# Block maxima of the weight quantiser by five halvings, exponents one chunk sooner, the step partly on ScalarE

## The reference, cut to what matters

```python
def _quant_elem(x, mbits):
    e = floor(log2(max(abs(x), 2**-30)));  e = max(e, 0)
    step = exp2(e - mbits)
    q = round(x / step) * step
    return clip(q, -max_norm, max_norm)

def _mx_quant(x, mbits):                      # weights: mbits = 1, max_norm = 6
    amax = max(abs(block of 32))
    shared_exp = floor(log2(amax)) - 2
    return _quant_elem(x / 2**shared_exp, mbits) * 2**shared_exp
```

## Time and profile before

| | |
|---|---|
| median of 3 runs | 1184.11 us (1183.37 to 1185.51) |
| profiled execution | 1184.98 us |
| its span | 1183.2 us |
| TensorE matmul busy | 1107.2 us (94%) |
| VectorE busy | 868.7 us (73%) |
| ScalarE busy | 606.5 us (51%) |
| GpSimd busy | 490.8 us (41%) |
| mean granted TensorE clock | 0.975 |

### The profile page before, as it was taken

The page is one execution under the profiler, slowest core; times in us unless marked ns, Lnnn a source line. Parts: engine busy times, 40 slices in busy tenths (PEclk is TensorE's granted clock), DMA queues, the critical chain, the costliest instruction groups (busy, mean ns, idle before and its releaser), DMA issues.

```text
span 1183.2 us, 17698 instructions
## 1 busy us (share of the span) xinstructions
PE 1107.2 (94%) x5878; PEld 885.2 (75%) x5878; DVE 868.7 (73%) x1471; ACT 606.5 (51%) x1236; POOL 490.8 (41%) x360
## 2 busy tenths in 40 slices
PE   3976868999999999999999999999899999999998
PEld 2433333477888888888888888887888989897887
DVE  6999989867867777786867777657666676765534
ACT  2523443545656556565656656553665565663110
POOL 1361000124555645564655645462656555550000
PEclk9797998999999999999999999999999999999999
DMA  9364135220010011101010010141103020111221
GB/s 324 129 199 166 45 126 194 89 85 18 19 56 29 23 53 31 53 18 58 18 58 27 22 35 14 63 123 54 55 19 83 28 55 35 48 36 72 71 106 71
DMA packets 41812, 83.10 MB, mean 70 GB/s; under 512 B 10211, under 2 KB 18916, under 8 KB 38564
## 3 DMA queue, kind: packets, MB, share of 16 engines
q1 hardware_dynamic: 40164, 77.24, 19.9%
q0 software_dynamic: 1600, 5.24, 1.4%
HBM read 71.59 MB, written 10.22 MB: 69 GB/s over the span
## 4 chain that ended last, share of the span: by engine, by line
PE 77%; DVE 11%; ACT 4%; issue 4%; DMA 2%; POOL 2%; SPq 1%; ACTq 0%; DVEq 0%; POOLq 0%
PE PS L1888 20%; PE PS L1890 20%; PE PS L1889 20%; PE PS L2037 10%; PE PS L1831 1%; PE PS L1674 1%; PE PS L1655 1%; ACT arena L970 1%; DVE blkamax L1177 1%; DMA arena<-in_ctx 1%; PE PS L1785 1%; PE PS L1725 1%; PE PS L1842 1%; DVE blkamax L1202 1%; DMA X<-in_x 1%
## 5 line engine op out<-in xcount | busy, mean ns | idle before, releaser
L674 POOL TENSOR_TENSOR arena<-arena,rsum 128x768 f32<-128x768 f32 x192 | 283.2, 1476 | 362.5 <-DVE rsum L1470 362.5
L985 ACT ACTIVATE PTH<-PS 128x384 fp32r<-128x384 f32 x384 | 167.7, 489 | 249.5 <-PE PS L2037 249.2
L1465 DVE TENSOR_REDUCE nmax<-PS 128x1 f32<-128x768 f32 x192 | 183.0, 954 | 116.2 <-PE PS L1890 115.0
L1515 DVE TENSOR_TENSOR PTL<-PS,PTH 128x384 fp32r<-128x384 f32 x384 | 194.5, 548 | 11.1 <-ACT PTH L985 10.4
L970 ACT ACTIVATE arena<-PS,nmax 128x768 f32<-128x768 f32 x192 | 174.2, 907 | 32.8 <-DVE nmax L1465 32.3
L2037 PE MATMUL PS<-identf,arena 128*128 128x128 f32 x1152 | 158.3, 273 | 5.8 <-POOL arena L674 3.6
L2037 PEld LDWEIGHTS PS<-identf,arena 128*128 128x128 f32 x1152 | 130.3, 140 | 9.3 <-POOL arena L674 4.4
L659 POOL TENSOR_TENSOR WQL<-arena,WQH 128x512 fp32r<-128x512 f32 x44 | 58.2, 1324 | 64.2 <-ACT WQH L744 64.2
L1888 PE MATMUL PS<-PTH,VSH 128*128 128x512 f32 (+1 forms) x198 | 81.1, 410 | 0.4 <-DVE X L1492 0.4
L1890 PE MATMUL PS<-PTH,VSL 128*128 128x512 f32 (+1 forms) x198 | 76.5, 386 | 0.0
L1888 PE MATMUL PS<-WOH,OTH 128*128 128x512 f32 (+1 forms) x180 | 74.7, 415 | 1.6 <-DVE OTL L1549 0.7
(11 more groups left out here) (289 smaller groups left out, 2540.9 us busy)
## 6 DMA issues: line engine op xcount, KB each, us to landing
arena<-in_wo SPq DMA_DIRECT2D x12, 1024.0 KB, 4.8
arena<-in_wq SPq DMA_DIRECT2D x44, 256.0 KB, 2.6
arena<-in_expert_w SPq DMA_DIRECT2D x8, 1024.0 KB, 4.8
arena<-in_wgu SPq DMA_DIRECT2D x11, 512.0 KB, 5.2
arena<-v_dram SPq DMA_DIRECT2D x8, 384.0 KB, 3.5
arena<-in_wd SPq DMA_DIRECT2D x4, 704.0 KB, 4.7
arena<-in_ctx SPq DMA_DIRECT2D x4, 512.0 KB, 4.0
arena<-in_ctx_t SPq DMA_DIRECT2D x2, 1024.0 KB, 10.6
```

The lines of the kernel that those rows point to most:

```text
L674: pool.tensor_tensor(PR[:, u % 4, :], PR[:, u % 4, :], rsum[:, u % 4:u % 4 + 1].broadcast_to([P, KEYS]), ALU.mult).then_inc(s["pn_ready"], 1)
L985: act.activation(fr(PTH[:, (u // 4) % 2, 3 * half:3 * half + 3, u % 4 * P:(u % 4 + 1) * P]), bank(B_PT[half])[:, 0:3 * P].rearrange("p (k ...
L1465: dve.tensor_reduce(nmax[:, slot:slot + 1], SC[pair][:, 0:KEYS], AX.X, ALU.max, negate=True)\
L1515: dve.tensor_tensor(fr(PTL[:, (u // 4) % 2, ks, cols]), bank(B_PT[half])[:, 0:3 * P].rearrange("p (k c) -> p k c", k=3), PTH[:, (u // 4) % ...
```

## The change

The reduce `weight_top` goes. `weight_halves` runs five times for a chunk (32 to 16, 8, 4, 2, 1); the fifth writes `block_top` and raises `amax_ready`. Halvings 0 to 4 of chunk c + 1 are laid around the shift, the rounding and the two caps of chunk c. The exponents of chunk c + 2 follow the fifth halving of chunk c + 1 and stand before its step and grid, so they are one chunk sooner than before. From chunk 5 on (`STEP_ON_ACT = 5`, the sixth chunk) ScalarE makes the step, ahead of the caps; for chunks 0 to 4 VectorE still does. In step 0, whose shift and rounding are done inside the layer norm, the exponents of chunk 1 still come first.

```diff
--- before.py
+++ after.py
@@ -328,6 +328,8 @@
 
         CONTEXT_LATE = ((10, 11, 12), (13, 14, 15))
 
+        STEP_ON_ACT = 5
+
         TAPS_AT = {9: 0, 10: 1, 11: 2, 12: 3}
 
         KPAIRS = KV1 // 2
@@ -346,8 +348,10 @@
         def tops(c):
 
             n, (t, _) = CHUNKS[c], chunk_blocks(c)
-            half, quarter = (top_scratch[int(c >= NCH)][:, a:b] for a, b in ((0, n // 2), (n // 2, 3 * n // 4)))
-            return [ap.rearrange("p (t e b) -> p t e b", t=t, e=MX >> i + 1) for i, ap in enumerate((half, quarter))]
+            scratch = top_scratch[int(c >= NCH)]
+            levels = [scratch[:, a:a + (n >> i + 1)] for i, a in enumerate((0, n // 2, 0, n // 2))]
+            return [ap.rearrange("p (t e b) -> p t e b", t=t, e=MX >> i + 1) for i, ap in enumerate(levels)]\
+                + [of_blocks(block_top[c % 2], c).unsqueeze(2)]
 
         def of_blocks(ap, c):
 
@@ -784,6 +788,9 @@
                 act.wait_ge(s["amax_ready"], c + 1)
                 if c >= 2:
                     act.wait_ge(s["wq8_ready"], c - 1)
+                if c >= STEP_ON_ACT:
+                    act.activation(of_blocks(block_step[c % 2], c), of_blocks(block_top[c % 2], c), ACT.Copy, scale=0.25)\
+                       .then_inc(s["step_ready"], 1)
                 for cap, sign in zip(block_caps[c % 2], (1.0, -1.0)):
                     act.activation(of_blocks(cap, c), of_blocks(block_top[c % 2], c), ACT.Copy, scale=1.5 * sign)\
                        .then_inc(s["caps_ready"], 1)
@@ -1194,24 +1201,18 @@
                 dve.scalar_tensor_tensor(w, weight_magic(c), ROUND / 2, w, ALU.mult, ALU.subtract)\
                    .then_inc(s["wx_shifted"], 1)
 
-            def weight_top(c):
-
-                if c >= 2:
-                    dve.wait_ge(s["caps_ready"], 2 * (c - 1))
-                dve.wait_ge(s["tops_ready"], 2 * c + 2)
-                dve.tensor_reduce(of_blocks(block_top[c % 2], c), tops(c)[1].rearrange("p t e b -> p t b e"),
-                                  AX.X, ALU.max).then_inc(s["amax_ready"], 1)
-
             def weight_halves(c, i):
 
-                src = tops(c)[0] if i else interleaved(weight_magic(c), c)
+                src = tops(c)[i - 1] if i else interleaved(weight_magic(c), c)
                 n = MX >> i + 1
                 if i:
-                    dve.wait_ge(s["tops_ready"], 2 * c + 1)
+                    dve.wait_ge(s["tops_ready"], 4 * c + i)
                 else:
                     dve.wait_ge(s["wexp_ready"], c + 1)
+                if i == 4 and c >= 2:
+                    dve.wait_ge(s["caps_ready"], 2 * (c - 1))
                 dve.tensor_tensor(tops(c)[i], src[:, :, 0:n, :], src[:, :, n:2 * n, :], ALU.max)\
-                   .then_inc(s["tops_ready"], 1)
+                   .then_inc(s["amax_ready" if i == 4 else "tops_ready"], 1)
 
             def weight_rounded(c):
 
@@ -1247,22 +1248,28 @@
             def weight_step(c, begun=False):
 
                 ahead = c + 1 < len(CHUNKS)
+                if begun:
+                    weight_exponents(c + 1)
                 if ahead:
-                    weight_exponents(c + 1)
+                    weight_halves(c + 1, 0)
                 if not begun:
                     weight_shifted(c)
                 if ahead:
-                    weight_halves(c + 1, 0)
+                    weight_halves(c + 1, 1)
                 if not begun:
                     weight_rounded(c)
                 if ahead:
-                    weight_halves(c + 1, 1)
+                    weight_halves(c + 1, 2)
                 weight_capped(c, 0)
                 if ahead:
-                    weight_top(c + 1)
+                    weight_halves(c + 1, 3)
                 weight_capped(c, 1)
                 if ahead:
-                    weight_least(c + 1)
+                    weight_halves(c + 1, 4)
+                    if c + 2 < len(CHUNKS):
+                        weight_exponents(c + 2)
+                    if c + 1 < STEP_ON_ACT:
+                        weight_least(c + 1)
                     weight_grid(c + 1)
 
             def act_quant(dst, src, n, q8, natural, transposed_parts=0):
@@ -1292,9 +1299,8 @@
 
 
             weight_exponents(0)
-            weight_halves(0, 0)
-            weight_halves(0, 1)
-            weight_top(0)
+            for i in range(5):
+                weight_halves(0, i)
             weight_least(0)
             weight_grid(0)
             dve.wait_ge(s["x_in"], 16)
```

## The result

The changed kernel took 1186.87 us (median of 20 runs, 1184.07 to 1189.44) against 1184.64 for the kernel before in as many runs on the same chip: ratio 1.0018, 95% interval 1.0012 to 1.0024. It is slower by 2.2 us, where 1183.9 and "no change that a measurement can tell" were forecast. The profiled execution took 1186.43.

What follows compares the result with a forecast made beforehand. The stage was taken to end by two paths 0.23 apart, VectorE's own and chunk 13's maxima through ScalarE to TensorE. Early lateness of 3.8 is repaid, the stage ends 0.2 to 0.3 early: 1183.9 us, range 1181.4 to 1187.2.

Steps and rivals of the forecast that it cites:

- The steady saving: VectorE's weight chunks: three small halvings replace the reduce, 0.19 saved; with the step on ScalarE 0.38 a chunk from chunk 5.
- ScalarE's step: From chunk 5 on: hidden behind the exponents by 0.24; on chunk 14 the grid waits about 0.35.
- Exponents of chunk 4: Early stage: their load, awaited until 45.22, now holds up the power additions; TensorE's correlations start 4.4 late.
- Exponents of chunk 5: Ahead of the search for lags: load issued at 50.53, takes 4.5; search begins at 56.5, 4.0 late.
- rival 2: Third context tile's GpSimd instruction is held up, so chunk 5's load and all above come 1.75 later: 1185.6; chance 0.17.
- Caps of chunk 4: ScalarE's caps stand behind late transposes and contexts of chunk 2: done at 71.1, wanted at 70.4, 0.7 lost.
- The last taps: TensorE at the stage's end: start 125.3, idle 0.7 ahead, clock stays at 2.4 GHz, 5.4 instead of 7.01.
- The sum: Lateness of VectorE's shift: 3.8 at chunk 4, paid back to 0.0 at chunk 14; stage ends 0.2 to 0.3 early.

Runs made afterwards that it cites:

- early6_dvestep: early6 with STEP_ON_ACT = 99, so VectorE makes every step instead of ScalarE: 1182.12 us.
- never: The changed kernel, but the exponents stay in their old place for every chunk: 1185.48 us.
- late4: The changed kernel, but the exponents of chunk 4 alone stay in their old place: 1184.93 us.
- after_again: The changed kernel repeated unchanged, beside the others on the same chip: 1187.01 us.
- late5: The changed kernel, but the exponents of chunk 5 alone stay in their old place: 1185.13 us.
- before_again: The kernel before repeated unchanged, for a second profile of it: 1183.49 us.
- loads_before: The kernel before with the loads of chunks 4 and 5 one place sooner in SyncE's queue: 1185.29 us.
- expo_only: The kernel before with only the exponents moved one chunk sooner, reduce and step as before: 1191.17 us.
- loads_after: The changed kernel with the loads of chunks 4 and 5 one place sooner in SyncE's queue: 1180.81 us.
- early6: The changed kernel, but exponents move one chunk sooner only from chunk 6 on: 1181.60 us.
- caps_loads: The changed kernel with the loads of chunks 4 and 5 and ScalarE's caps of chunks 3 and 4 sooner in their queues: 1179.48 us.
- caps_loads6: early6 with the loads of chunks 4 and 5 and ScalarE's caps of chunks 3 and 4 sooner in their queues: 1180.34 us.

## Why the prediction was wrong in sign

**The steady saving: right.** Halvings of 0.22, 0.19 and 0.17 us were forecast as 0.22, 0.18 and 0.17, a chunk at 5.56 came out at 5.56, and from chunk 5 on the lateness falls by the forecast steps. The rule of the Trainium skill that spoke against the split (Perfetto Trace Analysis, Optimizing Scalar/DVE Operations) would have given 0.03 a chunk for it, an estimate from its 60 ns; early6_dvestep shows 0.13.

**ScalarE's step: right.** It hides behind the exponents, and never, where they don't follow the last halving, shows the wait that it costs without cover, 0.29 a chunk. The last grid waits 0.30, forecast 0.35 in all.

**Exponents of chunk 4: right.** 45.10 against the 45.22 taken over; the correlations began 4.3 late (47.86 against 43.54), forecast 4.4.

**Exponents of chunk 5: the step that failed.** The prediction's "the load was issued at 50.53 and takes 4.5" took the old issue time over. It was issued at 51.97, behind the third context tile, and landed at 56.44: 1.4 later, and the search started 5.4 late, not 4.0. This was rival 2, given 0.17. Its place came out, its price was near (1.75, measured 1.4), and its result lay 1.3 below the measured time (1185.6 and 1186.87). The old issue time rested on an instruction that fell into a gap of VectorE in both profiles of the kernel before, and the edit shifts everything around that gap; the trace of before had held up one of two such instructions, so about one half would have been a fairer chance. The gap, 0.40 us of waiting for caps, could be seen in the trace. From the VectorE timeline of the kernel before:

```profile
48.44 0.29 DVE L1213 TENSOR_TENSOR arena<-arena 128x256 bf16<-128x256 bf16 x1
49.13 1.49 DVE L1236 TENSOR_TENSOR arena<-arena 128x1024 bf16<-128x1024 bf16 x1 [0.40 <-ACT arena L788]
```

GpSimd began at 48.89, in that gap. In the changed kernel step, grid and additions stand between the awaited exponents and the shift of chunk 3 and push it from 45.83 to 48.06, so GpSimd, at 48.67, begins beneath the shift, and the rounding follows it without a gap. late4 takes the push away and has the forecast issue time back: the failed step hangs on the wait for chunk 4's load, which the prediction had right.

**A term that was missing.** The search itself was delayed 0.8 more: the copy of 128 by 5 at 60.24 took 1.00 us instead of 0.17, while GpSimd worked on the fourth tile. In after_again, where the copy started later against GpSimd, it took 0.43. From the POOL timeline of the changed kernel:

```profile
48.67 2.85 POOL L641 TENSOR_SCALAR arena<-arena,qconst 128x1024 bf16<-128x1024 f32 x1 [3.64 <-ACT arena L807]
60.02 1.19 POOL L641 TENSOR_SCALAR arena<-arena,qconst 128x1024 bf16<-128x1024 f32 x1 [3.64 <-ACT arena L807]
```

With 1.4 and 0.8 the shift of chunk 4 is 6.0 late instead of 3.8. (In after_again it is 6.1, from 1.4 of issue, 0.7 of a longer load and 0.3 of the copy.)

**Caps of chunk 4: no wait.** The 0.7 forecast didn't occur, because VectorE came 2.2 later to them than thought, at 72.61, and ScalarE had made them from 71.16 on. late5, with an earlier VectorE, shows that wait (1.54). So the sum: 3.8 + 1.4 + 0.8 = 6.0 at chunk 4; 3.8 of lateness and the 0.7 were to be paid back by chunk 14, 4.5 in all, and 4.5 was; 1.4 is left, by the unrounded starts.

**The last taps: the number right, the reason not borne out.** They were to take 5.4 instead of 7.01, and took 5.42; their start, 126.71, is 1.4 later than forecast, as is everything. The reason given was that TensorE would idle only 0.7 us ahead of them. It idled 1.25, and other runs speak against idle time as the cause:

| run | TensorE idle ahead of the last taps, us | granted clock in their first 3.5 us | they took, us |
|---|---|---|---|
| before | 2.03 of 2.80 | 0.54 | 7.0 |
| before_again | 1.75 of 2.52 | 0.59 | 7.1 |
| never | 1.98 of 2.76 | 0.56 | 7.1 |
| loads_before | 2.04 of 2.84 | 1.00 | 5.4 |
| expo_only | 2.15 of 2.95 | 1.00 | 5.4 |
| changed kernel | 1.25 of 2.00 | 1.00 | 5.4 |

Two runs that idled longest kept the clock. So the 1.6 us came as forecast, but what gave them is open, and as far as is shown it was luck.

**The sum.** 3.0 us lie between 1183.9 and 1186.87. The stage has 1.4 of them (1.17 late, forecast 0.25 early). Another 0.5 come from the starting point: the forecast was counted from the 1184.11 of three runs, and the kernel before had 1184.64 in twenty. About 1 is left.

**The rest of the kernel: open.** The stage accounts for 1.2 to 1.3 us, and the medians differ by 2.2 and 3.0. From the third layer norm's first normalised row to the fourth's, the profiles of unchanged or nearly unchanged code differ: 49.1 and 49.3 us in the two of the kernel before, 50.3 and 47.9 in the two of the changed one, 47.4 to 51.4 over all runs. How TensorE's granted clock falls there goes with it: between 200 and 220 us it is 0.83 in the four slowest (50.3 to 51.4) and 0.87 to 1.00 in the others. An example is the window of 206 to 212 us, first of the changed kernel's profile,

```profile
206.00:212.00 6.00, 4.59 (x15) 2.02 (x17) 5.79 (x7) 0.60 (x1) 0.00 (x0) 0.50 0.31 89
```

then of after_again's, the same program:

```profile
206.00:212.00 6.00, 4.70 (x28) 2.38 (x29) 5.79 (x7) 2.29 (x3) 0.00 (x0) 1.00 0.26 71
```

In every row of the table of runs the median comes out 0.2 to 1.8 us worse than the stage says. One profile for each run can't tell whether an earlier or later stage shifts the odds of such a clock drop, so 1.1 us of the first difference and 1.7 of the second are not explained.

## What to carry to other kernels

Before an operation that needs a load is moved forward in an in-order queue, find what now stands behind it, and take the load's issue time from its own chain, not from the old trace: it may hang on an instruction that the edit itself displaces. A saving per iteration that begins with a debt should be given only from the iteration on where its inputs are early (here one threshold, EARLY_FROM, worth 5.3 us: 1186.87 to 1181.60), or the loads should move with it. When a wait is removed, look at once at what lay hidden under it: here the loads, the caps of chunk 3 and those of chunk 4 were layered, and the lowest time came with all of them removed. And one wait can set up the next: the wait for chunk 4's load pushed VectorE's work over GpSimd's instruction, and by that delayed chunk 5's load.

## What the runs showed of the hardware that was not expected

**VectorE and GpSimd hold each other up, and who starts first decides.** GpSimd's rounding of the third tile, one 1024-column instruction, shows it in all 14 profiles. In seven (before, before_again, never, late4, loads_after, loads_before, early6_dvestep) it began while VectorE was idle or in the last 0.13 us of a halving, and took 1.19 to 1.20; the VectorE instruction behind it took 1.49 instead of 0.69. In five (changed kernel, after_again, early6, expo_only, late5) it began beneath a running shift, took 2.5 to 2.9, and ended with the halving behind the rounding, which took 1.05 to 1.13 instead of 0.22 to 0.28. In caps_loads it began 0.11 into one grid instruction, with copies out of PSUM behind, and took 1.65: the rest of the grid's slot, 0.5, and its own 1.19; caps_loads6 is alike (1.64). A VectorE copy of five columns took 1.00 for the same reason. The Trainium skill (SBUF — State Buffer, Who interferes with whom) says of the shared port that "Issue order, not op shape, decides who blocks", and these rows agree. What they add is that a run of VectorE instructions without a gap kept GpSimd out over more than one of them: in the changed kernel from 48.67, beneath the shift, until the rounding ended at 50.6.

**The reduce was no protection.** The same section of the Trainium skill says that VectorE's two-input operations hold up GpSimd's reads and a reduce never does; the prediction took from it that three more halvings make a hold likelier. In expo_only, with the reduce kept and no halving added, the third tile took 2.92. It was held over the shift and the rounding, which are two-input operations, so the trace agrees with the rule, but its use in the prediction was wrong: what counts is which instructions run when GpSimd begins.

**A result used at once costs 0.11.** An instruction directly behind the 1024-column one whose output it reads started 0.72 after it, elsewhere 0.60 to 0.61 (expo_only: grid, then shift; never: exponents, then halving).

**Idle time just before a product did not decide the clock.** Ahead of the last taps TensorE had run 5.4 us at 1.00, nearly without a pause, in every run of the table on the last taps. Then it idled 1.75 of 2.52 us in before_again and fell to 1.2 GHz for most of the first 3.5 us of the taps; in loads_before it idled 2.04 of 2.84 and stayed at 2.4 GHz. Two executions of one kernel (before and before_again) also differ in the correlations: 11.1 us in the one, mostly at the lower level, and 6.8 at the upper level in the other. What decides is not shown.
